# Two-layer graph network with layer norms, one core: last quarter of the second layer by column halves, tail in groups of 4, 2 and 2 blocks

## What is computed

```
h1, h2 = 3-layer relu MLPs of (1+1+eps) * (adj @ x), the same for x2     # adj 4096x4096, x 4096x128
x = layernorm(x + concat(h1, h2) @ Wm.T + bm)
A = adj + I;  d = rsqrt(rowsum(A))                                        # second layer
x = layernorm(x + (d[:,None] * A * d[None,:]) @ x @ W.T + b)
```

## Time and profile before

| | |
|---|---|
| median of 3 runs | 613.05 us |
| the profiled execution | 613.1 us, span 611.3 us |
| PE busy | 590.3 us, 97% of the span |
| DVE busy | 545.6 us, 89% |
| ACT busy | 368.2 us, 60% |
| DMA | 141.55 MB, mean 232 GB/s; 330 to 400 GB/s in the second layer |
| last quarter of the second layer | unit 0 starts on PE at 553.31, unit 28 at 593.93, the last product at 601.56 |
| tail behind the last product | 601.56 to 611.3 |

### The profile page before, as it was taken

How to read it: one execution, slowest core, us unless ns; L and a number is a source line. 1 busy time by engine, 2 the same in 40 slices (tenths; PEclk the granted TensorE clock), 3 DMA queues, 4 the chain that set the end, 5 groups by cost and what they waited for, 6 DMA issues and landing times.

```text
span 611.3 us, 7947 instructions
## 1 busy us (share of the span) xinstructions
PE 590.3 (97%) x2636; PEld 478.9 (78%) x2636; DVE 545.6 (89%) x696; ACT 368.2 (60%) x443; POOL 28.1 (5%) x30
## 2 busy tenths in 40 slices
PE   4999999999999999999999999999989999999994
PEld 3888888888888888888888888858668778778873
DVE  5999989998987997998899999876898998998994
ACT  5555337752545773453675254685767797797781
POOL 1000000001100000200000110001100100000011
PEclk9999999999999999999999999999999999999998
DMA  8967555334555433455533576583978999999800
GB/s 292 414 234 281 205 203 206 138 138 138 207 206 183 161 137 137 169 191 191 204 137 137 206 275 248 172 335 139 339 283 346 342 399 363 349 380 371 333 34 36
DMA packets 21289, 141.55 MB, mean 232 GB/s; under 512 B 2320, under 2 KB 2832, under 8 KB 5008
## 3 DMA queue, kind: packets, MB, share of 16 engines
q1 hardware_dynamic: 20544, 139.15, 61.1%
q10 hardware_dynamic: 720, 2.10, 0.9%
HBM read 139.14 MB, written 2.10 MB: 231 GB/s over the span
## 4 chain that ended last, share of the span: by engine, by line
PE 85%; DVE 10%; ACT 2%; issue 2%; DMA 1%; POOL 1%; POOLq 0%; SPq 0%; DVEq 0%; ACTq 0%
PE ps L344 75%; DVE alo L636 7%; PE pd L362 6%; PE pd L373 2%; PE pd L405 1%; ACT ahi L489 1%; DMA raw<-a_t 1%; DVE stats L708 1%; DVE z L801 1%; POOL rstd L896 1%; ACT outn L519 1%; PE ps L418 0%; DVE mv L716 0%; DVE raw L791 0%; DVE x1lo L775 0%
## 5 line engine op out<-in xcount | busy, mean ns | idle before, releaser
L489 ACT ACTIVATE ahi<-raw 128x1024 fp32r<-128x1024 f32 x255 | 267.7, 1059 | 209.3 <-PE ps L344 203.3
L636 DVE TENSOR_TENSOR alo<-raw,ahi 128x1024 fp32r<-128x1024 f32 x255 | 307.3, 1217 | 46.3 <-ACT ahi L489 45.3
L344 PE MATMUL ps<-ahi,x1hi 128*128 128x512 f32 x504 | 162.9, 399 | 12.1 <-DVE alo L630 8.0
L344 PE MATMUL ps<-ahi,x2s 128*128 128x512 f32 x512 | 159.9, 391 | 0.0
L344 PE MATMUL ps<-alo,x1hi 128*128 128x512 f32 x504 | 158.5, 391 | 0.0
L344 PE MATMUL ps<-ahi,x1lo 128*128 128x512 f32 x504 | 158.4, 391 | 0.0
L344 PEld LDWEIGHTS ps<-ahi,x1hi 128*128 128x128 f32 x504 | 92.5, 189 | 40.8 <-issue 14.1
L344 PEld LDWEIGHTS ps<-ahi,x2s 128*128 128x128 f32 x512 | 96.7, 189 | 20.3
L344 PEld LDWEIGHTS ps<-ahi,x1lo 128*128 128x128 f32 x504 | 94.9, 188 | 20.2
L344 PEld LDWEIGHTS ps<-alo,x1hi 128*128 128x128 f32 x504 | 95.0, 188 | 19.9
L344 PE MATMUL ps<-alo,x2s 128*128 128x512 f32 x256 | 80.6, 391 | 0.0
(11 more groups left out here) (66 smaller groups left out, 265.7 us busy)
## 6 DMA issues: line engine op xcount, KB each, us to landing
raw<-a_t SPq DMA_DIRECT2D x124, 1024.0 KB, 4.8
raw<-a_t SPq DMA_DIRECT2D x7, 512.0 KB, 8.9
xn<-x SPq DMA_DIRECT2D x3, 1024.0 KB, 7.9
out<-outn ACTq DMA_DIRECT2D x3, 512.0 KB, 3.9
par<-params SPq DMA_DIRECT2D x1, 708.0 KB, 14.3
xn<-x SPq DMA_DIRECT2D x2, 256.0 KB, 4.8
raw<-a_t SPq DMA_DIRECT2D x2, 256.0 KB, 5.1
xn<-x SPq DMA_DIRECT2D x1, 512.0 KB, 8.2
```

The lines of the kernel that those rows point to most:

```text
L344: mm = pe.matmul(ps[bank][:, :], block_of(w, n), a[c], start=(n == 0 and k == 0), stop=(n == JB - 1 and k == 2))
L489: act.activation(ahi[:, n % SPLIT, :], raw_tile(layer, n), ACT.Copy).then_inc(hi_ready, 1)
L636: dve.tensor_tensor(alo[:, n % SPLIT, :], raw_tile(layer, n), as_f32(ahi[:, n % SPLIT, :]), ALU.subtract).then_inc(lo_ready, 1)
```

## The change

The whole last quarter of the second layer is cut by columns first. A unit is now two contraction blocks by 512 columns, so again 128 x 1024 elements, three plus three products of 512 columns. Units 0 to 15 give columns 0 to 511 (`ps0`), units 16 to 31 columns 512 to 1023 (`ps1`). The loads for it are two DMAs of 512 KB per pair of units, in pieces of 2 KB. The order of the contraction blocks is set so that the squares for the identity, two in a unit, lie in units 4, 5 and 20, 21. PE asks for `alo` only at a unit's third product.

After unit 19, ACT has copied `ps0` and PE projects blocks 0 to 3. Of units 28 to 31 PE first takes columns 512 to 767 (into `ps1`), then columns 768 to 1023 (into `ps2`), in products of 256 columns. Units 30 and 31 have buffers of their own (`hhi`, free by then, and `alo_extra`), so ACT doesn't wait for PE there. ACT copies `ps1`; DVE adds `ps2` onto its second half. The tail runs in groups of blocks 0 to 3, 4 and 5, 6 and 7; SP issues their stores.

```diff
+QUADS = tuple((0, 1, LAST * 2 + c) + tuple(m for m in range(2, JB // 4) if m != LAST * 2 + c) for c in range(CH))
+EXTRA = JB - 2
+TW = CW // 2
+TAIL = ((0, 4), (4, 6), (6, 8))
...
+            c, i = n // HALF_UNITS, n % HALF_UNITS                      # unit(n)
+            return c, 4 * QUADS[c][i // 2] + 2 * (i % 2)
...
+            for m in range(PAIRS):                                      # SP
...
+                for r, done in enumerate((unit_in[s], landed)):
+                    sp.dma_start(dst[:, r, :].rearrange("p (t w) -> p t w", w=CW),
+                                 a_t[pair + r][:, :, c * CW:(c + 1) * CW]).then_inc(done, 16)
+            for g, (k0, k1) in enumerate(TAIL):
+                sp.wait_ge(tail_ready[g], 1)
+                sp.dma_start(out[LAST][:, k0 * P:k1 * P], outn[:, k0 * P:k1 * P]).then_inc(tail_written, 16)
...
-            def last_products(q):                                       # PE
...
+            def unit_products(n, cols, open_bank, bank, opens, closes):
...
+                for t in range(2):
+                    at = slice(t * CW + cols.start, t * CW + cols.stop)
+                    for k, (w, a) in enumerate(((x1hi, hi), (x1lo, hi), (x1hi, lo))):
+                        if open_bank and t == 0 and k == 2:
+                            pe.wait_ge(lo_ready, (QUARTERS + LAST) * JB + n + 1)
+                        mm = pe.matmul(bank, block_of(w, j + t), a[:, at], start=(n == opens and t == 0 and k == 0),
+                                       stop=(n == closes and t == 1 and k == 2), skip_group_check=True)
...
+                    if n == PE_PROJECT:
+                        project(LAST - 1)
+                    if n == HALF_UNITS + PE_PROJECT + 2:
+                        project(LAST, 1, range(KB // CH))
+                for half in range(2):
                     for n in range(JB - SPLIT, JB):
...
+                        mm = unit_products(n, slice(half * TW, (half + 1) * TW), half == 0, ps[1 + half][:, 0:TW],
+                                           (None, JB - SPLIT)[half], JB - 1)
...
+                            if n == JB - SPLIT + 1:
+                                project(LAST, 2, range(*TAIL[1]))
...
-                wait(act, block_used, q * JB + (layer * QUARTERS * JB + n + 1 - SPLIT))
+                if not (last and n >= EXTRA):
+                    wait(act, block_used, q * JB + (layer * QUARTERS * JB + n + 1 - SPLIT))
+                act.activation(ring_hi(n, last), raw_tile(layer, n), ACT.Copy).then_inc(hi_ready, 1)
...
+                        if q == LAST and n == HALF_UNITS + SPLIT - 1:   # ACT
+                            act.activation(h[:, 0, :], ps[0][:, :], ACT.Copy).then_inc(ay_copied, 1)
...
+            for g, (k0, k1) in enumerate(TAIL):                         # DVE
+                if g == 2:
+                    dve.wait_ge(ay_copied, LAST * CH + 3)
+                    dve.wait_ge(block_used, 2 * QUARTERS * JB)
+                    dve.tensor_tensor(h[:, 1, TW:CW], ps[2][:, 0:TW], h[:, 1, TW:CW], ALU.add).then_inc(ay_added, 1)
+                residual2(LAST, g, range(k0, k1), k1 - 1, k0)
```

More of the change, by code:

```diff
@@ L158, in build @@
         raw2_in = [sem(f"raw2_in{i}") for i in range(RAW2)]
+        unit_in = [sem(f"unit_in{i}") for i in range(RAW + RAW2)]
         x_hi = sem("x_hi")
@@ L310, in _ @@
             load2(3)
[L311 removed]
+            turns = groups * RAW // (RAW + RAW2)
+            with sp.Fori(1, turns - turns // QUARTERS) as g:
                 for s in range(RAW + RAW2):
@@ L408, in project @@
                 mm.then_inc(project_done, 1)
-            def last_products(q):
-                for c in range(CH):
-                    for n in range(JB - SPLIT, JB):
[L414 to L420, removed]
+            def unit_products(n, cols, open_bank, bank, opens, closes):
+                c, j = unit(n)
+                hi, lo = ring_hi(n, True), ring_lo(n, True)
+                for t in range(2):
[5 more added lines that the diff above has]
+                                       stop=(n == closes and t == 1 and k == 2), skip_group_check=True)
+                return mm
@@ L432, in empty @@
                         wait(pe, ay_copied, before * CH + (bank + 1))
-                last = isinstance(q, int) and q == QUARTERS - 1
-                for n in range(JB - SPLIT if last else JB):
+                for n in range(JB):
                     if before is None and n % KB == 0:
@@ L602, in _ @@
                 layer1_quarter(q, q - 1)
[L604 to L613, removed]
+            act.wait_ge(ay_done, LAST + 1)
+            act.activation(h[:, 1, 0:TW], ps[1][:, 0:TW], ACT.Copy).then_inc(ay_copied, 1)
+            act.activation(h[:, 1, TW:CW], ps[1][:, TW:CW], ACT.Copy).then_inc(ay_copied, 1)
+            act.wait_ge(out_written, 16 * LAST)
+            for g in range(2):
+                act.wait_ge(norm_ready, 2 * QUARTERS + g)
+                for k in range(*TAIL[g]):
+                    i = act.activation(to_outn(k), z[:, k, :], ACT.Identity,
+                                       scale=rstd[:, k:k + 1], bias=nshift[:, k:k + 1])
+                i.then_inc(tail_ready[g], 1)
         @block.vector
@@ L791, in add_identity, with add_identities_last, residual2 @@
                 dve.tensor_tensor(square, square, identity[:, :], ALU.add).then_inc(identity_added, 1)
-            def residual2(q, half, blocks, whole):
-                if blocks[0] == half * HB:
+            def add_identities_last(n):
+                wait_unit(dve, n)
+                for at in squares_of(n):
+                    square = raw_tile(1, n)[:, at:at + P]
+                    dve.tensor_tensor(square, square, identity[:, :], ALU.add).then_inc(identity_added, 1)
+            def residual2(q, half, blocks, whole, first=0):
+                if blocks[0] == first:
                     dve.wait_ge(project_done, q + (1 + half))
@@ L919, in _ @@
                 norm_power(q + QUARTERS + 1)
-            for half in range(2):
-                norm_power(2 * QUARTERS + half, slice(half * HB, (half + 1) * HB))
+            for g, (k0, k1) in enumerate(TAIL):
+                norm_power(2 * QUARTERS + g, slice(k0, k1))
 _OUT = (N, P)
```

125 lines of the change are left out of this document (89 added, 36 removed).

## The result

The changed kernel takes 608.98 us (median of 4 runs, 608.15 to 609.65) against 613.04 for the one before (4 runs, 611.93 to 613.65). The ratio is 0.9939, 95% interval 0.9926 to 0.9953: faster, by 4.1 us as the difference of the medians and by 2.9 to 4.5 us by the interval. The forecast was 610.3, faster; the time lies 0.2 us under the low end of its range, 609.2.

The account below looks back on a forecast made before the run. PE, busy 97% of the span, was taken as the bound, with DVE at 89%. From 613.1 us, 0.8 gained up to the last product and 2.0 in the tail, less 0.05, gave about 610.3; range 609.2 to 612.8.

Parts of the forecast that it names:

- Squares at units 17 and 18: Four identity squares on DVE there, 0.20 us each, delay `alo` of unit 19: PE stalls 0.2 us.
- The projection: Blocks 0 to 3 projected after unit 19 cost PE 0.81 us, the same as in the old place.
- I let it swallow the whole 0.6 us of stalls: The moved projection gives DVE and ACT time before the `outn` stretch, removing PE's 0.6 us of stalls by unit 28.
- The loads: Two 512 KB DMAs in 2 KB pieces cost nothing, over 14 us in hand, until a pair takes 3.6 us (290 GB/s).
- Products of 256 columns: In units 28 to 31 on PE, taken as 0.12 us each, bounds 0.10 and 0.19.
- Rival (a): Weight loads set the pitch of the short products at 0.19 us: 613.2 us, no change; chance 0.10.
- Units 30 and 31: ACT isn't held by PE there; DVE's pitch of 1.16 us from unit 26 puts the last subtraction at 597.1.
- DVE and PE arrive nearly together: Before the addition of `ps2`: DVE's second group ends at 601.4, PE's result is there at 601.2.
- The tail: Three groups in a row on DVE, the last of two blocks: 9.3 us after PE's last result become 7.3.
- Rival (d): The tail's split does nothing, since each group has fixed waits: 611.9 us; chance 0.14 together with (b).
- theory S: From the follow-ups: squares leaving units 21 to 28 removed PE's 0.6 us of stalls; put back, 0.3 to 0.8 us returns.

Follow-up runs that it names:

- squares_late: Changed kernel with the second half's identity squares moved from units 20, 21 to units 24, 25: 608.51 us, ratio 0.9934 to the kernel before the change.
- lo_first: Changed kernel with PE asking for `alo` before a unit's first product instead of its third: 609.44 us, one run.
- project_late: Changed kernel with the projection of blocks 0 to 3 moved back behind unit 29 of the last pass: 611.42 us, one run.
- whole_loads: Changed kernel with the last quarter's adjacency stored in the new order, one 1 MB DMA in 8 KB pieces per pair: 609.16 us, ratio 0.9941 to the kernel before.
- kb1_loads: Changed kernel with the last quarter's loads in 1 KB pieces, four DMAs of 256 KB per pair of units: 608.42 us, one run.
- no_extra: Changed kernel without own buffers for units 30 and 31, which use the ring of four: 609.00 us, ratio 0.9940 to the kernel before the change.
- split_384: Kernel with squares in units 24, 25, plus last columns cut 384 and 128, tail groups of 4, 3, 1: 609.72 us, ratio 0.9953 to the kernel before.
- tail_44: Changed kernel keeping the column quarters, but with tail groups of 4 and 4 blocks: 610.68 us, ratio 0.9972 to the kernel before the change.
- squares_in_outn: Changed kernel with the first half's projection late, PE asking for `alo` first, second-half squares in units 26, 27: 612.23 us, one run.

## Why the prediction was right, point by point

- **Direction and mechanism: right.** From the mark 3.5 us were gained where 2.8 were forecast. Times in the profiled execution, forecast first: unit 28 at 594.3, measured 594.73; last subtraction 597.1, 597.15; addition 601.45, 601.47; z of the last group 602.7, 602.69; its variance done 604.2, 604.31; `outn` from 605.3, 605.12; end 608.5, 607.9. Unit 28 was late by 0.3 us behind the mark (0.2 by the squares, 0.1 by the projection), but the last subtraction, which the pass over columns 512 to 767 waits for, came as forecast.
- **Squares at units 17 and 18**: forecast 0.2 us of stall, measured 0.37 in unit 19. squares_late gives back 0.43 us, lo_first shows that without the later question it would be 0.46 us more. The term was too small by half.
- **The projection**: 0.81 us taken, 0.9 measured. The other 0.1 is the idle time in unit 20, which squares_late has too and project_late has not.
- **"I let it swallow the whole 0.6 us of stalls"** (the projection): the amount was right, and the mechanism holds: the stall is ACT's, and PE comes late enough not to meet it. In squares_late, with squares in the stretch, `alo` of unit 26 is there 34.78 us from the mark and PE starts the unit at 35.35. But the projection isn't the only thing that does it. project_late has no stall either, since the squares' own 0.37 us and the later question cover it. The forecast didn't see this second cover.
- **The loads**: cost nothing, right; whole_loads and kb1_loads show it from both sides. What was in hand was less than forecast, 9.9 us or more where I had over 14, since a load lands 7.0 us after issue and not 4.8. The Trainium skill's rule of at least 1 MiB a DMA (DMA: Bandwidth & Descriptors, Bandwidth) isn't borne out here: transfers of 256 KB moved 349 GB/s, 84% of the 415 of the earlier trace rows, with some eight in flight (an estimate, from 6.1 us to landing at that rate). The page's figures in that section are for DMAs issued from GpSimd, these are issued from SP.
- **Products of 256 columns**: 0.12 taken, 0.12 measured. Rival (a) is out: each load still lasts 0.19 us, but they overlap.
- **Units 30 and 31**: I let DVE's pitch set the last subtraction and not the buffers. That was right: without them it comes only 0.17 us later (no_extra).
- **"DVE and PE arrive nearly together"**: right (601.56 and 601.27 before an addition at 601.47), and split_384 shows what it means: with one block moved from the last group to the one before, DVE comes 0.9 us behind PE.
- **The tail**: forecast 7.3 us from PE's last result to the end, measured 6.6. Two terms were mis-sized: the power, kept at its time for four columns (1.12 with signals), took 0.81; from `outn` to the end, kept at 2.58, took 2.1 us. They are 0.3 and 0.4 us. The last group took 0.1 more from z to its variance (602.69 to 604.31, forecast 1.5), since the sum left out its shift, 0.15. Together that is the miss of 0.6. (The other 0.7 of the 1.3 us between 610.3 and the median is the profiled execution's own distance from it.) Of the second, tail_44 has 2.5 us with a store of 256 KB by SP, and the kernel before 2.6 with one by ACT, so most of it is the store's size, little the change of queue. Rival (d) is out by tail_44.

## What to carry to other kernels

A tail of dependent small steps costs by the work in its last group, so cut the last group and not only the products that feed it, but stop where the shorter products no longer get cheaper and the engine that does the steps has no time left between groups. When small extra steps are moved off an engine's busy stretch, look at where they land: four squares of 0.2 us cost 0.43 us beside the means and nothing where the engine waits for ACT anyway. When a stall is gone, ask first whether PE now only comes later: follow the instruction that ended the stall, and not the idle time alone. Both outcomes that theory S forecast came true, and the timelines of ACT and DVE contradict it. And take times of such stretches from a mark behind the part that didn't change, since whole runs scatter by more than most of what is compared here.

## What the runs showed of the hardware

- Products with a weight load each, by moving columns: 512 in 0.227 us, 384 in 0.174, 256 in 0.12, 128 in 0.11 us, at a granted clock of 1.00.
- The power on POOL depends on its columns even when they are few: 128x4 in 1.01 us, 128x3 in 0.85, 128x2 in 0.69, 128x1 in 0.55.
- Loads in pieces of 8, 2 and 1 KB, from 560 to 580 us: 345, 382 and 349 GB/s. Only the last is what the DMA engines could do (share 1.10, and the loads fell behind); the one of 8 KB has a share of 0.88. I had expected 250 to 330 for 1 KB.
- From the end of the last `outn` to the end of the span: 2.1 us with a last store of 128 KB, 2.5 with 256 KB, both issued by SP.
- The granted clock can fall to its lower level within the tail while PE waits (squares_in_outn): four products of 128 columns then took 1.23 us against 0.71.
